# A graph layer with linear attention: the key state by rounded products, with splits and later roots off VectorE and ScalarE

## The reference

```python
xn = _layernorm(x, axis=-1)                       # x: 1250 x 512
x = x + _L0_gnn_ref(xn, edge_index, ...) + _L0_mix_ref(xn[None], ...)[0]
x = x + _L0_ffn_ref(_layernorm(x, axis=-1)[None], ...)[0]

# _L0_mix_ref: linear attention, 8 heads of 64
q = _feature_map(x @ Wq + bq)                     # elu(t) + 1
k = _feature_map(x @ Wk + bk)
v = (x @ Wv + bv)
kv = jnp.einsum('bshd,bshe->bhde', k, v)
z = 1.0 / jnp.einsum('bshd,bhd->bsh', q, k.sum(axis=1))
out = jnp.einsum('bshd,bhde,bsh->bshe', q, kv, z) @ Wp + bp

# _L0_gnn_ref: 20000 edges, sorted by dst
agg = jax.ops.segment_sum(x[src], dst, num_segments=N)
h = (1.0 + eps) * x + agg                         # then two layers with batch norm
```

## Time and profile before

| | |
|---|---|
| median of three runs | 577.58 us (577.13 to 579.36) |
| the profiled execution | 576.5 us, its span 574.7 us |
| TensorE busy | 525.4 us (91%) |
| VectorE busy | 347.9 us (61%) |
| ScalarE busy | 267.0 us (46%) |
| GpSimd busy | 88.5 us (15%) |
| mean granted clock of TensorE | 0.985 |

### The profile page before, as it was taken

The page is one execution under the profiler, slowest core; times in us unless marked ns, Lnnn a source line. Parts: engine busy times, 40 slices in busy tenths (PEclk is TensorE's granted clock), DMA queues, the critical chain, the costliest instruction groups (busy, mean ns, idle before and its releaser), DMA issues.

```text
span 574.7 us, 8366 instructions
## 1 busy us (share of the span) xinstructions
PE 525.4 (91%) x2745; PEld 361.7 (63%) x2745; DVE 347.9 (61%) x977; ACT 267.0 (46%) x562; POOL 88.5 (15%) x93
## 2 busy tenths in 40 slices
PE   1779999999999999999999999975799999998897
PEld 0334544455478888799999999863454555454445
DVE  4887787777876555548886222595344444353577
ACT  2889778667654534036664222342333333433200
POOL 4001011100000000000000000004324444445200
PEclk9999999999999999999999999996899999999899
DMA  8500000000020007283008202997989999999768
GB/s 307 188 1 2 1 1 1 1 1 0 2 74 0 1 1 259 108 314 117 2 6 342 98 32 75 390 377 233 337 303 417 416 414 413 415 415 416 310 245 326
DMA packets 31257, 105.70 MB, mean 184 GB/s; under 512 B 4912, under 2 KB 10033, under 8 KB 23404
## 3 DMA queue, kind: packets, MB, share of 16 engines
q1 hardware_dynamic: 21212, 86.09, 38.8%
q0 software_dynamic: 4880, 9.78, 4.5%
q10 hardware_dynamic: 5120, 9.26, 4.4%
HBM read 93.49 MB, written 17.84 MB: 194 GB/s over the span
## 4 chain that ended last, share of the span: by engine, by line
PE 72%; DMA 9%; SPq 6%; ACT 4%; DVE 4%; issue 4%; ACTq 1%; DVEq 0%; POOL 0%; POOLq 0%
PE PS L519 8%; PE PS L518 8%; PE PS L520 8%; SPq L1538 6%; PE PS L593 6%; DMA BIG<-in_we 6%; PE PS L793 5%; PE PS L808 5%; PE PS L556 5%; PE PS L548 4%; PE PS L622 4%; PE PS L623 4%; PE PS L735 3%; PE PS L582 3%; PE PS L782 1%
## 5 line engine op out<-in xcount | busy, mean ns | idle before, releaser
L518 PE MATMUL PS<-ROUND 128*128 128x416 f32 (+3 forms) x232 | 83.8, 361 | 0.0
L519 PE MATMUL PS<-ROUND 128*128 128x416 f32 (+3 forms) x232 | 83.5, 360 | 0.0
L520 PE MATMUL PS<-ROUND 128*128 128x416 f32 (+3 forms) x232 | 83.4, 359 | 0.0
L808 PE MATMUL PS<-BIG 128*64 128x512 f32 x216 | 51.1, 593 | 1.2 <-DVE BIG L1206 0.6
L1041 DVE BATCH_NORM_STATS2 BST<-BIG 128x6 f32<-128x416 f32 (+1 forms) x36 | 20.7, 590 | 43.8 <-ACT BIG L1388 35.2
L622 PE MATMUL PS<-ROUND 128*128 128x416 f32 (+3 forms) x120 | 43.5, 363 | 2.3 <-DVE ROUND L958 1.8
L518 PEld LDWEIGHTS PS<-ROUND 128*128 128x128 f32 (+1 forms) x232 | 43.5, 188 | 2.6
L520 PEld LDWEIGHTS PS<-ROUND 128*128 128x128 f32 (+1 forms) x232 | 43.5, 188 | 2.5
L942 DVE TENSOR_TENSOR BIG<-PS,BIG 128x280 f32 (+17 forms) x69 | 30.7, 445 | 23.7 <-PE PS L582 18.9
L519 PEld LDWEIGHTS PS<-ROUND 128*128 128x128 f32 (+1 forms) x232 | 43.5, 188 | 2.4
L1432 ACT ACTIVATE BIG<-PS,BIG 128x256 f32<-128x256 f32 x32 | 15.1, 473 | 61.4 <-PE PS L793 33.2
(11 more groups left out here) (261 smaller groups left out, 954.2 us busy)
## 6 DMA issues: line engine op xcount, KB each, us to landing
BIG<-in_we SPq DMA_DIRECT2D x50, 1024.0 KB
XA<-in_we SPq DMA_DIRECT2D x6, 1024.0 KB
y_rows<-KVB SPq DMA_DIRECT2D x19, 256.0 KB
BIG<-y_rows SPq DMA_DIRECT2D x9, 512.0 KB, 8.0
EXTRA<-in_we SPq DMA_DIRECT2D x4, 1024.0 KB
BIG<-in_we SPq DMA_DIRECT2D x8, 512.0 KB
BIG<-in_wqkvp ACTq DMA_DIRECT2D x3, 1024.0 KB, 14.8
XA<-in_x SPq DMA_DIRECT2D x9, 256.0 KB, 8.9
```

The source lines that it names most:

```text
L518: mm(o, ah, bh, start=first, stop=False)
L519: mm(o, ah, bl, start=False, stop=False)
L520: return mm(o, al, bh, start=False, stop=last)
L808: ins = mm(PS[64 * j:64 * j + 64, b, :], HT[:, s, 128 * f2 + 64 * j:128 * f2 + 64 * j + 64], buf[:, 1024 + 512 * f2:1024 + 512 * f2 + 512] ...
```

## The change

- `gmm` multiplies rounded halves: three matmuls (`products`) of `XNH`, `XNL` with `PHIH`, `PHIL`, where it had one in float32. It waits for `xl` and `phl` of its tile.
- `xh` moves ahead, to just behind the transposes of its tile; `xl` moves from VectorE in the aggregation to GpSimd in the key stage.
- New: `phh` (ScalarE, a cast of the mapped keys) and `phl` (GpSimd, what is left). `kadd` of tile i waits for `phl` of tile i - 4 where it waited for the products.
- The key map is one Exp on ScalarE, and the clamp takes the minimum with 1 as well: max(u, min(e, 1)). The query map is changed in the same way, three activations to two.
- Roots of batches 2 and 3 are made on GpSimd by Newton's steps (`nwt`, 14 instructions that each wait for the one before) in place of ScalarE's root and VectorE's reciprocal.
- The second preparation of the edges' check (`prep 1`, VectorE) is due at 50 and not at 17; some scratch moves to other columns, and -bq is no longer made.

```diff
--- before.py
+++ after.py
+ROOTS = 2
+NEWTON = 14
...
-    at(17.0, "prep", 1)
+    at(50.0, "prep", 1)
...
-        at(8.3 + 1.7 * (b - 1) + 0.5, "sq", q)
-        at(8.3 + 1.7 * (b - 1) + 0.9, "rr", q)
+        at(8.3 + 1.7 * (b - 1) + 0.5, "sq" if q < ROOTS else "nwt", q)
+        at(8.3 + 1.7 * (b - 1) + (0.9 if q < ROOTS else 5.0), "rr", q)
...
         at(k + pair / 2 + 2.4, "phi", i)
-        at(k + pair / 2 + 3.2, "xh", i)
+        at(k + pair / 2 + 3.2, "phh", i)
+        at(k + pair / 2 + 3.6, "phl", i)
+        at(xt + 1.6, "xh", i)
+        at(xt + 2.2, "xl", i)
...
+        PHIH, PHIL = ([rounded(QT0 + 1024 * q + 512 * h, 512) for q in range(4)] for h in range(2))
...
                     if k == 0:
-                        pe.wait_ge(s_phi, i + 1)
-                    ins = mm(PS[:, 4 + k, :], XN[0:n, i, 128 * k:128 * k + 128], PHI[i % 4][0:n, :], start=(i == 0),
-                             stop=(i == NT - 1))
+                        pe.wait_ge(s_xl, i + 1)
+                        pe.wait_ge(s_phl, i + 1)
+                    f = slice(128 * k, 128 * k + 128)
+                    ins = products(PS[:, 4 + k, :], XNH[0:n, i, f], XNL[0:n, i, f], PHIH[i % 4][0:n, :], PHIL[i % 4][0:n, :],
+                                   i == 0, i == NT - 1)
...
-                    dve.wait_ge(s_sq, step[1] + 1)
-                    link(V.reciprocal(RR[:, q], RR[:, q]))
+                    if step[1] < ROOTS:
+                        dve.wait_ge(s_sq, step[1] + 1)
+                        link(V.reciprocal(RR[:, q], RR[:, q]))
+                    else:
+                        dve.wait_ge(s_nwt, NEWTON * (step[1] - ROOTS + 1))
...
-                        dve.wait_ge(s_g, i - 3)
+                        dve.wait_ge(s_phl, i - 3)
...
-                    V.tensor_tensor(u, u, w, ALU.max).then_inc(s_phi, 1)
+                    V.scalar_tensor_tensor(u, w, 1.0, u, ALU.min, ALU.max).then_inc(s_phi, 1)
...
-                elif kind == "xl":
-                    i, n = step[1], rows(step[1])
-                    dve.wait_ge(s_xh, i + 1)
-                    if i < NT - 1:
-                        dve.wait_ge(s_g, i + 1)
-                    else:
-                        b, use = plan["gts"][3]
-                        dve.wait_ge(full[b], use)
-                    V.tensor_tensor(XNL[0:n, i, :], XN[0:n, i, :], XNHf[0:n, i, :], ALU.subtract).then_inc(s_xl, 1)
...
+                elif kind == "phh":
+                    i, n = step[1], rows(step[1])
+                    act.wait_ge(s_phi, i + 1)
+                    if i >= 4:
+                        act.wait_ge(s_g, i - 3)
+                    A.copy(PHIH[i % 4][0:n, :], PHI[i % 4][0:n, :]).then_inc(s_phh, 1)
...
-                    A.activation(w, u, ACT.Relu, bias=ONE[0:n, :], scale=-1.0).then_inc(s_kr, 1)
-                    act.wait_ge(s_kr, i + 1)
-                    A.activation(w, w, ACT.Exp, scale=-1.0).then_inc(s_ke, 1)
+                    A.activation(w, u, ACT.Exp, bias=NEG1[0:n, :]).then_inc(s_ke, 1)
...
-                    A.activation(e1, PS[:, b, 0:w], ACT.Relu, bias=NBQ[:, r:r + 1], scale=-1.0).then_inc(s_qr, 1)
+                    A.activation(e1, PS[:, b, 0:w], ACT.Exp, bias=bq[:, r:r + 1]).then_inc(s_qe, 1)
                     A.activation(QT[:, r, o:o + w], PS[:, b, 0:w], ACT.Identity, bias=BQ1[:, r:r + 1]).then_inc(moved[b], 1)
-                    act.wait_ge(s_qr, m + 1)
-                    A.activation(e1, e1, ACT.Exp, scale=-1.0).then_inc(s_qe, 1)
...
+                elif kind == "xl":
+                    i, n = step[1], rows(step[1])
+                    b, use = at_of(("xt", i))
+                    pool.wait_ge(s_xh, i + 1)
+                    pool.wait_ge(full[b], use)
+                    G.tensor_tensor(XNL[0:n, i, :], XN[0:n, i, :], XNHf[0:n, i, :], ALU.subtract).then_inc(s_xl, 1)
+                elif kind == "phl":
+                    i, n = step[1], rows(step[1])
+                    pool.wait_ge(s_phh, i + 1)
+                    G.tensor_tensor(PHIL[i % 4][0:n, :], PHI[i % 4][0:n, :], PHIH[i % 4].bitcast(F32)[0:n, :],
+                                    ALU.subtract).then_inc(s_phl, 1)
+                elif kind == "nwt":
+                    q, w = slice(*BATCH[step[1]]), BATCH[step[1]][1] - BATCH[step[1]][0]
+                    v, t, half, y = NWV[:, 0, 0:w], NWV[:, 1, 0:w], NWV[:, 2, 0:w], RR[:, q]
+                    done = NEWTON * (step[1] - ROOTS)
+
+                    def newton(ins):
+                        nonlocal done
+                        done += 1
+                        ins.then_inc(s_nwt, 1)
+                        pool.wait_ge(s_nwt, done)
+
+                    pool.wait_ge(s_st, BATCH[step[1]][1])
+                    newton(G.tensor_scalar(v, MV[:, q, 1], 0.5, 0.5e-5, ALU.mult, ALU.add))
+                    newton(G.tensor_scalar(y.bitcast(I32), v.bitcast(I32), -0.5, float(0x5f3759df - 2 ** 22), ALU.mult, ALU.add))
+                    for _ in range(3):
+                        newton(G.tensor_tensor(t, y, y, ALU.mult))
+                        newton(G.tensor_tensor(t, t, v, ALU.mult))
+                        newton(G.tensor_tensor(t, half, t, ALU.subtract))
+                        newton(G.tensor_tensor(y, y, t, ALU.mult))
```

More of the change, by code:

```diff
@@ L118, in front_schedule @@
         for i in range(NT):
-            if c == 0:
-                at(base + turn * i - 1.7, "xl", i)
             at(base + turn * i - 2.0, "conv", c, i)
@@ L310, in gnn_mix_moe @@
         BMV = sb("BMV", [128, 2, 8])
-        NBQ = sb("NBQ", [128, 4])
+        NEG1 = sb("NEG1", [128, 1])
         BQ1 = sb("BQ1", [128, 4])
@@ L354, in gnn_mix_moe @@
         WP = by(big(OH0, 2048), 4)
-        CHK, WCOL = by(big(KK0, 2 * ET).bitcast(I32), 2), big(KK0 + 3 * ET, ET)
+        CHK, WCOL = by(big(QT0 + 4100, 2 * ET).bitcast(I32), 2), big(QT0 + 4100 + 3 * ET, ET)
+        NWV = by(big(QT0 + 4900, 16), 4)
         SELB = big(XT0 + 9868, 128)
         KBI, REL, ORD = (big(XT0 + 9396 + ET * q, ET) for q in range(3))
-        FRWi = big(KK0 + 2 * ET, ET)[0:1, :].bitcast(I32)
+        FRWi = big(QT0 + 4100 + 2 * ET, ET)[0:1, :].bitcast(I32)
         ZR = [XG4[:, 0:418], KVB[:, :, :].rearrange("p r e -> p (r e)")[:, 0:418], XG4[:, 0:418]]
@@ L464, in gnn_mix_moe @@
         sd_ys = [sem(f"d_ys{q}") for q in range(NY)]
-        (s_pool, s_key, s_dif, s_oh, s_soa, s_sod, s_koh, s_st, s_sq, s_rr, s_xn, s_xh, s_xl, s_res0, s_kr, s_ke,
-         s_phi, s_ksum, s_g, s_ope, s_qr, s_qe, s_q, s_atr, s_agg, s_hth, s_htl, s_qz, s_qzl,
+        (s_pool, s_key, s_dif, s_oh, s_soa, s_sod, s_koh, s_st, s_sq, s_rr, s_xn, s_xh, s_xl, s_res0, s_ke,
+         s_phi, s_ksum, s_g, s_ope, s_qe, s_q, s_atr, s_agg, s_hth, s_htl, s_qz, s_qzl,
          s_kvt, s_mh) = (
             sem(n) for n in ("pool", "key", "dif", "oh", "soa", "sod", "koh", "st", "sq", "rr", "xn", "xh", "xl", "res0",
-                             "kr", "ke", "phi", "ksum", "g", "ope", "qr", "qe", "q", "atr",
+                             "ke", "phi", "ksum", "g", "ope", "qe", "q", "atr",
                              "agg", "hth", "htl", "qz", "qzl", "kvt", "mh"))
-        s_hot, s_xz = sem("hot"), sem("xz")
+        s_hot, s_xz, s_nwt, s_phh, s_phl = sem("hot"), sem("xz"), sem("nwt"), sem("phh"), sem("phl")
         (s_link, s_w1h, s_w1s, s_w2s, s_nv, s_ns, s_nb, s_relu, s_h1h, s_h1s, s_xst, s_rstd, s_nm, s_sel, s_par, s_lgz, s_ohs, s_lq,
@@ L877, in vector @@
                     dve.wait_ge(sd_vec, 16)
-                    V.tensor_scalar(NBQ[:, :], bq, -1.0, None, ALU.mult).then_inc(s_ope, 1)
                     V.tensor_scalar(BQ1[:, :], bq, 1.0, None, ALU.add).then_inc(s_ope, 1)
@@ L946, in vector @@
                     o, w = CH[c]
+                    b, use = at_of(("q", r, c))
                     dve.wait_ge(s_qe, 4 * c + r + 1)
-                    V.tensor_tensor(QT[:, r, o:o + w], QT[:, r, o:o + w], TMP[:, 2 * (r % 2) + 1, 0:w],
-                                    ALU.max).then_inc(s_q, 1)
-                elif kind == "xl":
-                    i, n = step[1], rows(step[1])
-                    dve.wait_ge(s_xh, i + 1)
-                    if i < NT - 1:
-                        dve.wait_ge(s_g, i + 1)
-                    else:
-                        b, use = plan["gts"][3]
-                        dve.wait_ge(full[b], use)
-                    V.tensor_tensor(XNL[0:n, i, :], XN[0:n, i, :], XNHf[0:n, i, :], ALU.subtract).then_inc(s_xl, 1)
+                    dve.wait_ge(moved[b], use)
+                    V.scalar_tensor_tensor(QT[:, r, o:o + w], TMP[:, 2 * (r % 2) + 1, 0:w], 1.0, QT[:, r, o:o + w], ALU.min,
+                                           ALU.max).then_inc(s_q, 1)
                 elif kind == "zr":
@@ L988, in vector @@
                     (b, use), (o, w) = plan["agg", c][f], CH[c]
-                    dve.wait_ge(s_ope, 3)
+                    dve.wait_ge(s_ope, 2)
                     dve.wait_ge(full[b], use)
@@ L1325, in scalar @@
```

(4 more changed lines are left out.)

## The result

| | before | the change |
|---|---|---|
| median of the runs taken side by side (four each) | 577.36 us (577.13 to 579.36) | 584.07 us (581.59 to 585.48) |
| the profiled execution, its span | 576.5, 574.7 us | 581.6, 579.8 us |
| first products of the query part | 114.5 us | 123.4 us |
| aggregation | 157.3 to 217.0 us | 165.2 to 223.2 us |
| mean granted clock of TensorE | 0.985 | 0.971 |

The change takes 1.0119 times as long [1.0095, 1.0143]: slower by 1.2%. The forecast was 579 and "within 0.5%" as the likeliest; the time is inside the range and on the slow side, between the third rival's 582 and the second's 587. The profiled execution is the quickest of its four. By stage, the query part begins 8.9 us late, where the sum had 3.6 (+0.9 + 1.5 + 1.2).

What follows compares the result with a forecast made beforehand. VectorE, stopped by GpSimd, was taken to be full and to bound the first 112 us. +0.9 + 1.5 + 1.2 - 2.3 = +1.3 on 576.5 gave 577.8, plus 1.1 for the median: 579 us, range 570 to 586.

Steps and rivals of the forecast that it cites:

- third rival: Key stage: GpSimd's work stops VectorE's clamps as well, +4.5 us in all, 582 us; chance 0.13.
- second rival: First 112 us: stops in full at 1.05 us each, Newton 4, hold 3; +9.8 us, 587 us; chance 0.22.
- Items 1 and 2: State products: 6.5 us less TensorE work; ScalarE loses four table loads (5.1 us) and 1.2 us over the key tiles.
- Item 3: GpSimd, key stage: 20 added subtractions at 1.28 us each; Newton's roots 4.2 us for a batch.
- Item 4: VectorE, 12 to 112 us: 20 stops of 0.80 us, 16.0 us, and Newton 2.0; VectorE full, +0.9 us.
- Item 5: Tile 1: Newton's batch 3 delays GpSimd's low half of keys, state products late by 3.8 us; +1.5 us.
- Item 6: Last tile: key sum and low half come before its state products, +1.2 us; tiles 2 to 8 have lead enough.
- Item 7: Aggregation: low halves of rows leave VectorE, so TensorE's waits of 1.78 and 0.48 us go; -2.3 us.
- Granted in full everywhere, so it plays no part: First two parts: the clock, granted in full in the kernel before, was given no part in the forecast.
- The first rival: First 112 us: VectorE's waits and evictions take the stops, 0.55 us each; -6.7 us, 571 us; chance 0.28.
- The signs I named: 12 to 112 us: VectorE 95% busy or more, 25 to 30 comparisons over 0.8 us, waits at tiles 1 and 9.

Runs made afterwards that it cites:

- Newton later: The change with both Newton batches moved behind the low halves of keys of tiles 0 and 1; 579.14 us, 1.0034 of the kernel before.
- The low halves ahead: The change with Newton's batches later and, in GpSimd's queue, each tile's low half of keys before its key sum; 575.23 us, 0.9954 of the kernel before.
- the spare subtractions: The kernel before with nineteen more GpSimd subtractions that nobody waits for; 580.57 us, 1.0064 of the kernel before.

## Why the prediction was right or wrong

**Items 1 and 2** held. Products start 0.23 us apart at full clock; one table load is left at the first Exp (1.28 us, L1317), and ScalarE is busy 24.1 us of the first stretch where it was 33.2:

```profile
L1317 ACT ACT_TABLE_LOAD x1 | 1.3, 1283 | 0.0
```

The Trainium skill, ScalarE: Activation LUTs, section What ACT_TABLE_LOAD costs, has this number for the load itself; the trace agrees.

**Item 3** held: 1.27 us for each low half of the keys, so that writing a rounded tile costs GpSimd nothing more (those of the rows take up to 1.85, see the third rival); Newton's 14 steps take 4.0 us where I said 4.2.

**Item 4** had the right size of the stops and not what came of it. The stops added 17.5 us where I had 16.0: 0.88 for each of the twenty subtractions, where I had 0.80. VectorE was forecast at 97 of 100 us and is at 87.3, since TensorE, held by GpSimd, leaves it without one-hot products: VectorE's waits for them include one of 5.0 us, the same hold:

```profile
DVE BIG L951 <- PE PS L589: 9.5, 7, 5.0
```

Where the holds are taken away VectorE is at 93 ("Newton later") and 94 ("The low halves ahead"), near what I wrote. Newton's steps, for which I took 2.0 us, stop nothing that can be measured: four comparisons of 180 columns beside them (32.16) took 0.78 us, as they did before (33.70).

**Item 5 is the step that failed**: "a hold by Newton" at tile 1, +1.5 us, bounds 0 and 3.8. At tile 1 it came as worked out: the low half ends 6.8 us after the clamp, for 6.9, and TensorE waits 2.79 us. But the order has batch 2 ahead of tile 0's low half in the same way, and the item puts that at nothing, without a reason. Batch 2 does not start when the statistics are there; it starts behind the low half of tile 1's rows, which waits to 27.77 for ScalarE. That is the hold of 5.0 us, and taking both away was worth 4.9 us in the median, above my upper bound of 3.8. How much of it is hold and how much is clock stays open, since no run has one without the other.

**Item 6** gave the key sum's place ahead of the low half a price at the last tile alone, +1.2, with 2.6 us of lateness; the wait there was 2.98. At the other tiles I counted on their lead, "enough for this". Once Newton was out of the way, putting the low halves first was worth 3.9 us more between the medians. In the traces TensorE's waits for the low halves fall from 5.2 to 3.5 us: that of tile 9 from 2.98 to 2.01, and two in the middle (0.45 and 0.25) are gone; the lower clock is granted for 3.4 us less. My reading of the middle tiles, which no run shows by itself, is that the stops had spent their lead, as VectorE makes their clamps late. I had costed the two effects one by one, and on one chain they can add.

**Item 7** held: both waits (1.78 and 0.48) are gone, the time from the query part to the end of the aggregation fell by 2.7 us where I had 2.3. The rest of the kernel did not shift in full, as I assumed, but took up 1.1.

**"Granted in full everywhere, so it plays no part"** was true of the kernel before, and not of the change: with the waits came 13.6 us at the lower level ahead of the query part.

**The rivals.** Two rivals lie nearer to the time than the forecast does: the third (582) by 2.1 us, the second (587) by 2.9, the forecast (579) by 5.1. Neither is what happened. The second wanted 1.05 us for each added subtraction and got 0.88, and a hold of 3. Its picture of key sum and low half back to back catching one comparison is what tile 8 shows. The third looked for clamps over 0.69 us; in the change none is, they take 0.68. But the contention it named is there, and here GpSimd pays for it:

```profile
88.07 1.85 POOL L1477 TENSOR_TENSOR ROUND<-BIG,ROUND 128x512 fp32r<-128x512 f32 x1 [6.46 <-ACT ROUND L1286]
...
88.11 0.68 DVE L916 SCALAR_TENSOR_TENSOR BIG<-BIG 128x512 f32<-128x512 f32 x1
```

1.85 us in place of 1.26, beside a clamp of usual length. In the trace of "Newton later" it is once the other way round, where the subtraction began 0.11 us ahead of the clamp (GpSimd, then VectorE):

```profile
65.35 1.34 POOL L1478 TENSOR_TENSOR ROUND<-BIG,ROUND 128x512 fp32r<-128x512 f32 x1 [6.18 <-ACT ROUND L1287]
```
```profile
65.46 1.78 DVE L917 SCALAR_TENSOR_TENSOR BIG<-BIG 128x512 f32<-128x512 f32 x1
```

So the third rival's clamp far over 0.69 us exists, one in the ten of that trace. The first rival, slack that takes the stops, is refuted by the spare subtractions: with nobody waiting for them they still cost 3.4 us, what the clock lost on the way included.

**The signs I named.** From 51 us on VectorE is full (95% or more), over the whole 100 us it is not (87.3). TensorE is not full there up to 101.7 us (46.6 of 50.6), and is in the last ten. 24 comparisons take over 0.8 us, for 25 to 30. Tiles 1 and 9 wait; the ninth step does not. The query part beginning after 120 was the sign of the second rival, and it does. The aggregation begins 7.9 us later, not 3 to 4.

So the time fell inside the range by its width. The sum was 3.8 us short on the profiled execution (+1.3 for 5.1); the largest term that it lacked is the hold at tile 0.

With its queue in another order the change is faster than the kernel before, by 2 us. So where the splits stand in GpSimd's queue decides whether it loses or gains. But they are dear in either case: without them, by the one Exp, Newton's roots and a later reciprocal, the gain is 6 us, and the reciprocal's wait is gone in both. The 6.5 us of TensorE that the rounded state products save are not worth what the splits cost in any order tried here.

## What to carry to other kernels

When work moves to an idle engine, walk that engine's queue from its first instruction, with start times read from what each one waits for, and ask at every instruction that somebody waits for what stands ahead of it: the order of the same instructions was worth 8.8 us here, more than the 3.4 us that as many subtractions cost where nobody waited for them. Put what nobody waits for yet (a running sum, roots for later tiles) behind what is waited for. And price a stop and a hold together if they lie on one chain, since the first can spend the lead that was to cover the second.
